# Routing tokens to experts inside the attention segments, in a four-layer decoder with three mixture-of-experts stages

## What is computed

```python
# after layer 1: 8 experts of width 512, the best one per token
probs = softmax(xt @ Wr + br);  gate, idx = max(probs), argmax(probs)
y = gate * (relu(xt @ W1[idx] + b1[idx]) @ W2[idx] + b2[idx])
# after layer 2: 16 experts of width 512, the best two per token, same form, summed
topv, topi = top_k(softmax(x @ Wr + br), 2)
# after layer 3: 31 experts of width 128 with gelu, the best three per token, and a shared one
vals, idx = top_k(softmax(x @ Wr + br), 3)
out = gelu(x @ ws1 + bs1) @ ws2 + bs2 + sum_j vals[j] * (gelu(x @ We1[idx[j]] + Be1[idx[j]]) @ We2[idx[j]] + Be2[idx[j]]) + x
x = layernorm(x + out)
```

## Time and profile before

| | us |
|---|---|
| median of three runs | 2506.84 |
| the profiled execution, own time | 2522.71 |
| its span, first to last instruction | 2520.9 |
| PE busy | 2059.6 (82%) |
| DVE busy | 1479.7 (59%) |
| ACT busy | 1162.7 (46%) |
| POOL busy | 590.5 (23%) |
| mean granted TensorE clock | 0.87 of full |
| segment 1 / expert stage 1 | 0 to 1032.6 / to 1145 |
| segment 2 / expert stage 2 | to 1734 / to about 1919 |
| group attention / segment 3 | to 2143 / to 2279.7 |
| expert stage 3 | to 2520.9 |

### The profile page before, as it was taken

How to read it: one execution, slowest core, us unless ns; L and a number is a source line. 1 busy time by engine, 2 the same in 40 slices (tenths; PEclk the granted TensorE clock), 3 DMA queues, 4 the chain that set the end, 5 groups by cost and what they waited for, 6 DMA issues and landing times. The chain is left out here.

```text
span 2520.9 us, 44062 instructions
## 1 busy us (share of the span) xinstructions
PE 2059.6 (82%) x15299; PEld 1045.7 (41%) x15318; DVE 1479.7 (59%) x3239; ACT 1162.7 (46%) x2245; POOL 590.5 (23%) x879
## 2 busy tenths in 40 slices
PE   4799999997799999577999999886495997895372
PEld 1233355543333334373554444443492344333252
DVE  5778766657887854256665646444256766437134
ACT  1477766562177765131565566742142442252041
POOL 4111112113411101233021111111540000202673
PEclk8799999999899999686998989887697999896586
DMA  4400011010101100161010100101591000100275
GB/s 146 188 27 27 27 40 38 22 29 1 51 27 32 28 15 16 48 228 51 27 39 22 28 21 11 37 16 50 171 339 38 1 1 1 45 17 17 66 215 150
DMA packets 135672, 148.30 MB, mean 59 GB/s; under 512 B 30033, under 2 KB 120593, under 8 KB 134174
## 3 DMA queue, kind: packets, MB, share of 16 engines
q1 hardware_dynamic: 97374, 100.77, 13.5%
q10 hardware_dynamic: 30272, 28.61, 3.5%
q0 software_dynamic: 7808, 16.10, 1.8%
HBM read 72.43 MB, written 26.99 MB: 39 GB/s over the span
## 5 line engine op out<-in xcount | busy, mean ns | idle before, releaser
L1413 ACT ACTIVATE probs<-psE 128x512 f32<-128x512 f32 (+2 forms) x1248 | 699.6, 584 | 410.6 <-PE psE L1150 189.5
L1550 DVE TENSOR_REDUCE maxima<-psM 128x2 f32<-128x1024 f32 (+4 forms) x640 | 677.7, 1081 | 350.7 <-PE psM L1220 137.6
L1243 PE MATMUL psE<-q_stack,k_stack 53*128 53x512 bf16 (+3 forms) x1152 | 372.8, 361 | 46.1 <-ACT probs L1413 35.5
L1220 PE MATMUL psM<-k_stack,q_stack 51*128 51x512 bf16 (+3 forms) x1280 | 351.6, 350 | 10.1 <-DVE maxima L1550 7.5
L1243 PEld LDWEIGHTS psE<-q_stack,k_stack 53*128 53x128 bf16 x1152 | 98.2, 94 | 244.4 <-ACT probs L1413 156.0
L1698 POOL TENSOR_SCALAR pool_t<-mean_var 128x4 f32<-128x4 f32 x60 | 15.0, 251 | 670.2 <-DVE mean_var L1475 666.5
L1220 PEld LDWEIGHTS psM<-k_stack,q_stack 51*128 51x128 bf16 x1280 | 102.6, 98 | 165.2 <-issue 89.7
L2254 POOL DMA_INDIRECT by_token<-probs,y_slot x148 | 141.8, 958 | 118.2 <-DVEq L2198 99.3
L2026 ACT COPY probs<-psE 128x128 f32<-128x128 f32 x148 | 39.4, 266 | 267.3 <-PE psE L1955 173.5
L1150 PE MATMUL psM<-masks_bf,ident_bf 64*128 64x128 bf16 (+2 forms) x832 | 156.4, 271 | 5.1 <-DMA k_stack<-k_parts 4.9
L1150 PE MATMUL psE<-masks_bf,ident_bf 64*128 64x128 bf16 (+2 forms) x960 | 156.9, 249 | 0.0
(11 more groups left out here) (477 smaller groups left out, 3610.0 us busy)
## 6 DMA issues: line engine op xcount, KB each, us to landing
q_stack<-q_parts SPq DMA_DIRECT2D x432, 64.0 KB
values<-experts_dram SPq DMA_DIRECT2D x40, 514.0 KB, 4.8
values<-experts_dram SPq DMA_DIRECT2D x79, 128.5 KB, 2.0
k_stack<-k_parts SPq DMA_DIRECT2D x156, 64.0 KB
hid<-experts_dram SPq DMA_DIRECT2D x15, 514.0 KB, 4.8
work<-experts_dram SPq DMA_DIRECT2D x15, 514.0 KB, 4.9
sorted<-hid ACTq DMA_DIRECT2D x7, 1024.0 KB, 10.7
c_values<-sorted ACTq DMA_DIRECT2D x78, 65.0 KB
```

The lines of the kernel that those rows point to most:

```text
L1220: out, len(heads), keys, lo, max_mask(c, t), lambda i, to, start, stop: nc.tensor.matmul(to, q_stack[lo:lo + R_MAX, job.a % Q_SLOTS, pair_ ...
L1243: lambda h, to, start, stop: nc.tensor.matmul(to, ks[lo:lo + R_END, pairs[h], k * P:k * P + c.kn], q_stack[lo:lo + R_END, job.a % Q_SLOTS, ...
L1413: nc.scalar.activation(probs[0:c.kn, m % 2, heads[0]:heads[-1] + 1, q0:S], psE[0:c.kn, n % 2, 0:len(heads) * (S - q0)].rearrange("p (h q) ...
L1550: nc.vector.tensor_reduce(top, psM[:, at:at + len(banks), 0:per * keys].rearrange("p b (h k) -> p b h k", h=per), AX_X, ALU.max, negate=Tr ...
```

## The change

**The routing moves into the segments.** Each chain gets a last job `Job("route")`. Its tasks are planned with the others: `logits` (PE), `pick_a` (DVE), `soft` (ACT), `pick_b` (DVE), `ranks` (PE), `slots` and `pages` (DVE), `stage`, `label` and `scatter` (POOL). In segments 1 and 2 they run batch by batch (`span` = 1), in segment 3 for two batches at a time (`span` = 2). State is carried from part to part: rows seen by expert (`before`), pages opened by expert (`tiles`), the first row of each expert's open page (`open_row`). Pages are numbered in the order in which they are opened, no longer by expert; `owner_i` holds the expert of each. The number of pages stays 23, 47 and 78.

**What is left in the expert stage.** Only the last part's scatters: 4, 8 and 24 where there were 16, 32 and 48. The tables `keep_i` and `dump_i` go; rows of a page that hold no token go to `by_token` rows below 2048, so `by_token` has (1+top)*2048 rows. `finished` has two DVE operations instead of three. Gates' transposes, bias matmuls and sums come after the page loop in stages 1 and 2, and in stage 3 inside it, with the shared expert, after pages 4, 12, 20 and 28 and the four that follow each.

**Row slots.** `X_SLOTS` goes from 7 to 12; loads stay five pages ahead, so that the load for page i+5 waits for `y_ready` of page i-7 and before and no longer for i-2; the wait for `t_full` goes. SP's wait for `placed` stands ahead of the third weight load instead of the fourth. The loads of the group attention's weights (2 MB, ACT's queue) stand at the start of stage 2 as before.

```diff
+    def route(self, job):
+        r, k = self.routing, len(self.routes)
...
+        for j in range(r.top):
+            self.put(self.ready[job.u] - 1.0 + j, "stage", job, j)
+        if k % r.span < r.span - 1:
+            return
+        job.part = self.routes[k + 1 - r.span:]
+        t = max(self.ready[j.u] for j in job.part)
+        self.put(t, "logits", job)
+        self.put(t + 1.5, "pick_a", job)
+        self.put(t + 2.3, "soft", job)
+        self.put(t + 2.8, "pick_b", job)
+        self.put(t + 6.0, "ranks", job)
+        self.put(t + 7.0, "slots", job)
+        self.put(t + 12.0, "pages", job)
+        self.put(t + 7.0, "label", job)
+        if k < B - 1:
+            for i in range(r.top * r.span * QT):
+                self.put(t + 12.0 + 1.1 * i, "scatter", job, i)
...
+            def stage_rows(self, me, k, u, j):
+                if j == 0 and self.reused(k):
+                    me.eng.wait_ge(self.placed, 16 * QT * self.top * k)
+                to = self.row_tile(k, j)
+                me.mark(nc.gpsimd.tensor_copy(to[:, :, 0:D], xt[:, u]))
+                me.mark(nc.gpsimd.tensor_scalar(to.bitcast(I32)[:, :, D + 1], col("ids", u * QT, (u + 1) * QT),
+                                                float((1 + j) * B * S), None, ALU.add))
...
+                me.mark(nc.vector.tensor_tensor(self.before, self.before, counted, ALU.add))
+                me.wait()
+                me.mark(nc.vector.tensor_tensor(rank, src[:, 0:self.G * n].rearrange("p (t e) -> p t e", e=n),
+                                                self.every(self.short), ALU.subtract))
...
-            W_SLOTS, X_SLOTS, Y_SLOTS = 5, 7, 5
+            W_SLOTS, X_SLOTS, Y_SLOTS, AHEAD = 5, 12, 5, 5
...
+            turned_at = {4 + 8 * u: u for u in range(B if shared else 0)}
+            shared_at = {i + 1: u for i, u in turned_at.items()}
+            biased_at = {i + 3: u for i, u in turned_at.items()}
+            summed_at = {i + 4: u for i, u in turned_at.items()}
...
-                        since(act, t_full, n - X_SLOTS + 1)
                         since(act, y_ready, n - X_SLOTS + 1)
...
-                        me.mark(nc.vector.tensor_tensor(to, x_row.bitcast(I32)[:, D + 1:D + 2], keep_i[:, i:i + 1],
-                                                        ALU.bitwise_and))
+                        me.mark(nc.vector.tensor_scalar(y_slot[:, i % Y_SLOTS, :],
+                                                        x_in[:, i % X_SLOTS, D + 1:D + 2].bitcast(I32),
+                                                        col("ids", i % (B * QT), i % (B * QT) + 1), None, ALU.max))
...
                 @block.gpsimd
                 def _(pool):
-                    pool.wait_ge(cleared, 16 * CLEARS)
-                    pool.wait_ge(copied, top)
-                    for j in range(top):
-                        pool.wait_ge(placeable, j + 1)
-                        for g in range(G):
-                            nc.gpsimd.indirect_dma_start(
-                                sorted_x, bass.IndirectOffsetOnAxis(ap=slot_i[:, j, g:g + 1], axis=0),
-                                rows_of[j][:, g, :], None).then_inc(placed, 16)
+                    for i in range(routing.G * top):
+                        routing.scatter(B - routing.span, i)
...
+        to1, to2, to3 = Routing(1, E1, K1, 1, False), Routing(2, E2, K2, 1, False), Routing(3, E3 - 1, K3, 2, True)
```

More of the change, by code:

```diff
@@ L143, in __init__ @@
         self.exp_time = 2.9 if not self.wide else {None: 11.3, "causal": 9.5, "tril2": 8.5}[masks]
-OPENS = ("q", "k", "v", "rq", "rk", "rows", "gather", "turn", "out", "back", "hidden")
+OPENS = ("q", "k", "v", "rq", "rk", "rows", "gather", "turn", "out", "back", "hidden", "logits", "ranks")
 def pair_and_half(c, g, j):
@@ L435, in needs @@
             return [("root", x, 1)]
+        if task in ("pick_a", "pick_b", "stage"):
+            old = self.routes[:self.routes.index(job)]
+        if task == "logits":
+            return [("back_evac", self.before[j]) for j in job.part]
+        if task == "pick_a":
+            return [("logits", x)] + [("pages", j) for j in old if j.part][-1:]
+        if task == "soft":
+            return [("pick_a", x)]
+        if task in ("pick_b", "label"):
+            return [("soft" if task == "pick_b" else "pick_b", x)] + [
+                ("stage", j, self.routing.top - 1) for j in job.part if task == "label"] + [
+                ("label", j) for j in (old if task == "pick_b" else []) if j.part][-1:]
+        if task == "ranks":
+            return [("pick_b", x)]
+        if task == "slots":
+            return [("ranks", x)]
+        if task == "pages":
+            return [("slots", x)]
+        if task == "stage":
+            return [("post_b", before)] + [("scatter", j, self.routing.top * self.routing.span * QT - 1)
+                                           for j in old if j.part and self.routing.reused(len(old))][-1:]
+        if task == "scatter":
+            return [("slots", x), ("label", x)]
         if task == "back":
@@ L544, in length @@
             return len(heads) * (S - x.job.att.first_q[k]) / 1200.0 + 0.17
+        if engine == "DVE" and task in ("pick_a", "pick_b", "slots", "pages"):
+            r = self.routing
+            one = 0.17 + r.span * QT * r.n / 960.0
+            return {"pick_a": 2 * one + 0.1, "pick_b": (3 + 7 * r.top) * one, "slots": 3.6 + 4 * one + 1.5 * r.top * one,
+                    "pages": 1.8 + (0.5 + r.top) * one}[task]
         if engine == "DVE":
@@ L1372, in _ @@
                                 tokens_out(pe, out, xT[:, job.u], w, bias).then_inc(full, 1)
+                        elif task == "logits":
+                            n, G = routing.n, routing.G
+                            for j in job.part:
+                                wait_freed(pe, plan.before[j], "back")
+                            out, full = bank_x(job, "logits")
+                            nc.tensor.matmul(out[:, 0:G * n].rearrange("p (t e) -> p t e", e=n), ones[0:3, :],
+                                             row(f"br{routing.li}").unsqueeze(1).to_broadcast([3, G, n]), start=True,
+                                             stop=False)
+                            for g in range(G):
+                                u, t = job.part[g // QT].u, g % QT
+                                tokens = xT_tiles[:, t, u] if routing.late else xT[:, u, t * P:(t + 1) * P]
+                                last = nc.tensor.matmul(out[:, g * n:(g + 1) * n], tokens, col(f"wr{routing.li}"),
+                                                        start=False, stop=g == G - 1)
+                            last.then_inc(full, 1)
+                        elif task == "ranks":
+                            pe.wait_ge(route_picked, routed_no["pick_b"][job])
+                            out, full = bank_x(job, "ranks")
+                            routing.rank_picks(out, route_at[job.part[0]]).then_inc(full, 1)
                         elif task == "back":
@@ L1923, in _ @@
[L1923 to L1928 removed]
+                    b_bank = [psM[:, 3, :], psM[:, 3, :]] if shared else [psE[:, 0, :], psE[:, 1, :]]
+                    g_bank = [psM[:, 3 if shared else u, :] for u in range(B)]
```

640 lines of the change are left out of this document (373 added, 267 removed).

## The result

The changed kernel takes 2496.0 us, median of eight runs, against 2510.0 us for the kernel before, median of eight runs beside them: a ratio of 0.9935, interval 0.9913 to 0.9958. The medians are 14 us apart; the ratio says 16 us faster (11 to 22), where 67 were forecast. The profiled execution of the change has a span of 2486.9 us and a clock of 0.895, that of before 2520.9 and 0.87; so the two profiles are 34 us apart where the runs are 16 apart, and the difference must be taken from single stretches, not from the spans.

The account below looks back on a forecast made before the run. PE was taken to bound the segments and the page loops of stages 1 and 2, nothing the gaps before pages. -100.8 + 26 + 2 + 6 = -66.8 us, from the runs' median 2506.8 to 2440 us, range 2410 to 2472.

Parts of the forecast that it names:

- The forecast's own sign of being wrong: A segment growing by over 15 us, tail scatters over 2 us, or stage 1 or 2 loops away from 1.9 us a page.
- What the change takes from the gaps: Between last `xT` and first page of stages 1, 2 and 3: 18.4, 37.5 and 44.9 us saved, 100.8 together.
- The early scatters: POOL's 24 in segment 3, 30 us of work, would end some 4 us ahead of the barrier and cost nothing.
- What it puts into the segments: Routing work and fills in the segments' tails: ends slip by 8, 8 and 10 us, 26 together, bounds 0 and 38.
- What moves within the stages: Gates' work after the pages costs 2 us in stages 1 and 2; with the shared expert, stage 3's loop 6.
- the unevenness of the lots: Stage 3's page loop: with work beyond PE's 11 us to spare in 32 pages, it costs 6 us, bounds 0 and 15.
- The slots and the third operation of `finished`: Twelve row slots and one DVE operation fewer in the page loops: nothing, bounds 0 and 5 us gained.
- Rival 1: Segment tails pay in full, slips 38 us instead of 26, stage 3's loop 15 instead of 6: 2472 us, chance 0.20.
- 11 us for the 53 last fills: Behind segment 3's last logits: fills hidden beside DVE's picks, but at the low clock stage 3 starts 11 us later.
- Rival 3: Early scatters held by DVE stand in front of roots on POOL: up to 148 us added, 2588 us, chance 0.04.
- Rival 4: Early scatters pile up on POOL, half still queued at the barrier: 38 us come back, 2478 us, chance 0.03.
- the rule that was weighed: A DVE tensor_tensor in SBUF does not hold scatters; an earlier 3.43 us scatter spoke against it, perhaps 0.3 us lost each.

Follow-up runs that it names:

- e3: The changed kernel with all routing inside the segments but only behind the last batch's transposes: 2535.9 us, 1.0092 of the kernel before.
- e2: The changed kernel without any fill from the first logits of each segment on: 2496.3 us, 0.9944 of the kernel before.
- e1: The changed kernel with each repeated run of fills written once, from the first logits of a segment on: 2479.4 us, 0.9886 of the kernel before.
- e6: The changed kernel with `pick_b`'s DVE operations done twice for every part but a segment's last: 2517.8 us, 1.0037 of the kernel before.
- e7: The changed kernel with stage 3's lots after pages 4, 22, 40 and 58 instead of 4, 12, 20 and 28: 2494.2 us, 0.9934 of before.
- e9: The changed kernel with each lot's bias and shared-down matmuls in quarters behind four pages: 2492.9 us, 0.9919 of the kernel before.
- e8: The changed kernel with seven row slots instead of twelve: 2494.9 us, 0.9940 of the kernel before.
- e5: e1 with DVE's routing in shorter pieces, put back up to 0.5 us for attention steps, and later logits: 2477.0 us, 0.9854 of the kernel before.

## Why the prediction was wrong

The direction was right and the size was not: 67 us forecast, 16 measured, outside the range. The forecast's own sign of being wrong, a segment that grows by over 15 us, came in segments 2 and 3. By its own steps:

- **What the change takes from the gaps** held: 18.4, 37.5 and 44.9 forecast, 17.1, 39.4 and 42.2 measured from `xT` to page (98.7 against 100.8). Stage 1's row load came 6.2 us behind the last scatter's start instead of 4.15. Stage 3's gap was 2.6 us over the forecast, and not by DVE: its chain took 26.4 us from the last `xT`, 28.2 were forecast. The early scatters, which were to end 4 us ahead of the barrier and cost nothing, end behind DVE. DVE's timeline:

```profile
2302.58 1.00 DVE L1317 TENSOR_REDUCE gates<-k_stack 128x248 f32<-128x744 f32 x1
```

and POOL's, the last scatter ahead of the barrier and the first behind it:

```profile
2304.11 0.96 POOL L1155 DMA_INDIRECT sorted<-values,slot_i  x1 [0.30 <-issue]
2308.97 0.96 POOL L1155 DMA_INDIRECT sorted<-values,slot_i  x1 [3.90 <-POOLq L119]
```

In ten of the eleven profiles of the change and its forms the first scatter of stage 3 comes 3.89 to 3.92 us after POOL's last early one, whether DVE ended 4.0 us ahead of POOL (e3) or 1.0 behind it (e2). In stages 1 and 2, where POOL had long been done, it comes 1.7 and 1.8 us after DVE's end. By that difference the queue on POOL cost stage 3 some 3.7 us, an estimate; no run took it away by itself.
- **What it puts into the segments** is the step that failed: slips of 8, 8 and 10 us with a bound of 38, measured 12.6, 30.5 and 22.1, 65. The text said that DVE has room on average, 40 of 100 us busy, and in segments 1 and 2 sized the slip from PE's fills instead. Both halves were wrong. The room on DVE is not where the routing lands: the chain xT of one batch, probabilities, division, projection, statistics, root, rows passes through DVE again and again, and a routing block starts whenever DVE is free for a moment. 70 us of DVE work were added and 65 came out at the end, 55 with the doubled fills gone (e1); doubled picks gave 24 and 25 (e6). The upper bound should have been all the DVE work added, which the forecast's own prices give: three parts at 8.6, three at 11.8 and one at 22.1 us, some 83 with nothing absorbed. In segment 3 it counted 20 us of DVE and put half of it "in front of something late"; the tail grew by 22.1 us, so as much as all of it came out at the end.
- The fills were the smaller part, and in another way: their number was read as idle time to be filled, and was in part the same time filled twice. That was 10 us (e1). The single ones cost next to nothing and keep the clock (e2).
- **What moves within the stages**: 1 us for each of the ends of stages 1 and 2. From the loop's last scatter to the next `xT` it is 18.8 us in the change against 18.6 in both profiles of before, and 22.3 against 23.4 and 22.5: nothing, or next to it. Stage 3's loop 6, measured 9 (106.3 against 97.4 and 97.6), for the reason that was given as "the unevenness of the lots" and not for the other, too little slack in 32 pages (e7, e9).
- The slots and the third operation of `finished` at nothing: right for the slots (e8); the operation was not tried by itself.
- With 65 for 26 and 9 for 6 the sum comes near: -100.8 + 65 + 2 + 9 = -25, against -16 with an interval to -22. The rest is not accounted for.
- Rival 1, the tails pay in full, was the right one for the tails, with too small a price, since its bound too came from the fills. Its 11 us for the 53 last fills did not come: they end at 2290.9, the last pick on DVE at 2291.8. Rival 3 did not come about: scatters in the tails are 0.95 to 1.23 us, and roots wait for at most two of them (2.2 us for batch 2's in segment 2, 1.5 for batch 3's in segment 3). Rival 4 did not either as it was meant: only the last part's scatters stood behind the barrier, but 18 of the 24 early ones of segment 3 ran after the last `xT`, at the price above.

Of the rule that was weighed: the hold of the earlier trace rows came back with short operations, and was as small as forecast. DVE's timeline of the changed kernel:

```profile
2298.25 0.93 DVE L1274 TENSOR_TENSOR k_stack<-k_stack 128x744 f32<-128x744 f32 x1
...
2301.57 0.97 DVE L1313 TENSOR_TENSOR k_stack<-k_stack 128x744 f32<-128x744 f32 x1
```

and POOL's at the same moments:

```profile
2298.90 1.12 POOL L1155 DMA_INDIRECT sorted<-values,slot_i  x1 [0.30 <-issue]
...
2301.58 0.96 POOL L1155 DMA_INDIRECT sorted<-values,slot_i  x1 [0.31 <-issue]
```

The first scatter begins within its operation and ends at 2300.02, 0.84 us after it, as those of rows 10 end 0.83 after theirs. The second begins 0.01 us after its operation and takes 0.96 us as if alone. This holds in all profiles of the study. Twenty-four scatters began 0.08 us or more after the start of a TENSOR_TENSOR on SBUF of 0.41 to 2.68 us that ran on beside them, and all ended 0.82 to 0.84 us after it (one 0.95). Fifteen that began within 0.03 us of such a start took 0.95 or 0.96. The scatter above loses 0.16 us, the longest loss in a form of the change is 0.48 (1.44 us, in e7 to e9). By the inference of the Trainium skill (SBUF — State Buffer, "Who interferes with whom") a tensor_tensor with both inputs in SBUF does not hold descriptor generation; the twenty-four speak against it. The moment of the start decides: L1314 of e3_late held a scatter that began 0.54 us into it and not one that began 0.03. Why that is so, the rows do not show.

## What to carry to other kernels

Work that is moved off a gap into a busy stretch must be priced on the engine that does it, in full, until the order shows that it lies beside waits and not in front of steps of the chain: an engine that is half idle on average can have no free microsecond. Work on the other engines that ends at the same barrier needs the same look: POOL's early scatters, thought to be covered by DVE, came out last in stage 3. If work must go into such a stretch, smaller pieces put behind the chain's own steps are worth trying (e5: 14 us gained in two tails, 5 lost in the third). And read a planner's output for the same idle time counted twice, before its fills are taken for time that was free.

## What the runs showed of the hardware beyond that

Without fills the granted clock in segment 1's tail fell from 1.00 to 0.68 and the tail took 81.7 us instead of 72.3, with DVE and ACT as busy as before (41.5 and 26.4 us against 41.7 and 26.2): 91 idle-time matmuls were worth 9 us there, and 12 against e1_once, where the doubled ones are gone and the clock is 1.00. In segments 2 and 3 the clock fell too, from 0.74 and 0.94 in e1_once to 0.67 and 0.77, and the tails did not get longer (78.3 and 60.2 us against 79.6 and 60.9). In a tail that waits for DVE a lower clock can cost nothing.
